# A fused attention, FFN and linear-attention kernel: a new step order in its linear phase, a split output projection and roots by Newton steps

## The chip, the cores and the metric

The kernel runs on one core of one Trainium2 chip. The metric is the device time of one execution in microseconds; lower is better. TensorE (PE) multiplies matrices and writes PSUM, VectorE (DVE), ScalarE (ACT) and GpSimd (POOL) do the elementwise work, SyncE (SP) issues DMAs. All engines run their own instruction queue in order and meet only at semaphores.

## The reference

A layer of four residual blocks on x of shape (2, 2048, 128): softmax attention, an FFN, a gated linear attention with 16 heads of width 64, and the FFN again. The change touches the third block:

```python
q = silu(x @ Wq); k = silu(x @ Wk); v = silu(x @ Wv)      # 16 heads of 64
q, k = l2norm(q), l2norm(k)
g = sigmoid(x @ Wf - dt_bias); beta = sigmoid(x @ Wb)
A = exp(-exp(A_log))
for t:                                                     # per batch and head
    o_t = (q_t @ state) * g_t
    state = A * state + beta_t * outer(k_t, v_t)
o = o * rsqrt(mean(o * o) + 1e-5) * norm_w
o = o * sigmoid(x @ Wg + bg)
x = x + o @ Wo
```

Here x is first normalized over its 128 channels.

## The kernel before

The linear phase (linear_phase, L1316 on) walks over NT = 16 tiles of 128 tokens, both batches at once, in steps m = -2 to 16. A step works on three tiles: it finishes tile m-1 (norm, output projection, residual), computes the recurrence of tile m, and prepares keys, values and queries of tile m+1. Within a tile a batch b has two chunks of 64 tokens; the recurrence inside a chunk is done by scores and attend, across chunks by recall (reading the 64x64 states) and update (products for the next state). Times in this text are in microseconds.

TensorE's jobs: by_feature makes q, f, g (f0 to f3 and so on, two 128x256 pieces each), by_token makes k, v (128x512). Both split their operands in a high and a low part and take three passes (three, L1443 to L1448). scores, attend, recall and update use quarters of the array (64x64); turn_k transposes k (64x128); sum_squares (128x32) adds the squares of q ("sq") and of the output u ("su"); turn_totals and turn_scales transpose; spread_scales (b0 to b3) spreads a head's scale over its features; project_out multiplies u with w_out in plain fp32 (L1588); turn_y and turn_x transpose.

The results go through four PSUM banks, ps0 to ps3, dealt out round by round in the order of the list in Ring: a job gets the bank of the job four places ahead of it, and free() lets TensorE wait until that job's reader is done. written() is the reader's wait for TensorE, taken() a wait for the reader. attend and recall share o_ps, update writes s_ps.

VectorE: decayed (scores times the decay table, L1735), new_state (L1797), gate_o (u = (f+1)o, L1783), gate_u (u = (gate+1)u, L1789), square_q (L1741), guard_q, add_totals and gather_totals (the sums of squares on their way to the root), scale_u (L1763), sum_k and guard_k (L1770, L1774), the layer norm's moments and normalize (L94 to L112), residual. ScalarE: silu of k, v, q (L1897, L1904), the tanh of f and g (L1916), squares (L1953, L1959), copies out of PSUM. GpSimd: decay_keys (L2079), decay_queries (L2086), fade (L2095), weigh_v (L2071), coefficients with a root by power of -0.5 (L2061), invert_totals with another such root and the split of its result into two parts (L2101 to L2106), low_x (L2052).

The order of each engine's work in a step is written out by hand in step(m) of that engine. TensorE's before:

```text
f0 be s0 f1 su k0 f2 sT k1 f3 v0 turn_k0 sq g0 k2 g1 k3 g2 sB g3 v1 b0-b3 attend v2 attend
project_out recall s1 v3 turn_y turn_x recall update q0 q1 attend turn_k1 attend q2 recall q3 recall update
```

(s0 and s1 are scores of batch 0 and 1, sT turn_totals, sB turn_scales, be the betas.)

## Time and profile before

| | us |
|---|---|
| median of 3 runs (914.35 to 917.34) | 914.47 |
| the profiled execution, its own time | 915.93 |
| its span, first to last instruction | 913.8 |
| PE busy | 841.7 (92%) |
| POOL busy | 636.4 (70%) |
| DVE busy | 548.9 (60%) |
| ACT busy | 511.6 (56%) |
| mean granted TensorE clock | 0.976 |

The linear phase fills the span from about 290 to the end; its steady steps lie between 345 and 830, and the last FFN overlaps its end. Busy times are averages over stages; what a step is bound by is read from a stretch of steps. In rows of the trace, DVE, ACT and POOL instructions that follow one another overlap by about 0.1 us, since an instruction's row reaches to its last write.

### The profile page before, as it was taken

The page shows a single profiled execution, that of the slowest core. Times are in us where ns is not written, and L with a number is a line of the kernel's source. Part 1 is how long each engine was busy: PE and PEld are TensorE (multiplying, and loading weights), DVE is VectorE, ACT ScalarE, POOL GpSimd, SP SyncE. Part 2 cuts the span into 40 slices and gives each one's busy share as a digit, 9 for nine tenths or more (in the row PEclk, how much of TensorE's full clock was granted, in tenths as well). Part 3 has the DMA queues.
Part 4 walks back from the last instruction along what each step waited for, and adds up shares of the span by engine and source line. Part 5 has one row for each costly group of instructions (what it writes and reads, how often), then busy time and mean ns, then how long its engine had stood idle before and what let it go on. Part 6 is the DMA issues. An engine that isn't in the chain of part 4 may idle for free. (4 is left out here: it accounts for less than half of the span.)

```text
span 913.8 us, 31013 instructions
## 1 busy us (share of the span) xinstructions
PE 841.7 (92%) x13152; PEld 717.5 (79%) x13152; DVE 548.9 (60%) x1247; ACT 511.6 (56%) x1105; POOL 636.4 (70%) x530
## 2 busy tenths in 40 slices
PE   4858998999797789999999999999999999998897
PEld 3648998899695678887888888888888888877786
DVE  3986566566684455655655655656556556666563
ACT  4745553565566636645646556566466467364354
POOL 3973211321455988898898898898898898988352
PEclk9998999999997889999999999999999999999999
DMA  5001000100100000000000000000000000000011
GB/s 189 25 13 34 25 12 1 31 19 1 25 1 1 1 3 3 3 3 3 3 3 2 3 4 2 3 4 2 3 3 3 4 2 3 4 1 3 3 36 57
DMA packets 19415, 12.36 MB, mean 14 GB/s; under 512 B 7760, under 2 KB 18768, under 8 KB 19024
## 3 DMA queue, kind: packets, MB, share of 16 engines
q1 hardware_dynamic: 19280, 10.39, 3.9%
q8 instruction: 105, 1.72, 0.8%
q14 instruction: 30, 0.25, 0.1%
HBM read 8.29 MB, written 2.10 MB: 11 GB/s over the span
## 5 line engine op out<-in xcount | busy, mean ns | idle before, releaser
L2101 POOL TENSOR_TENSOR la_scale<-la_scale,lt_mhalf 128x32 f32<-128x32 f32 x16 | 100.6, 6285 | 43.4 <-DVE la_scale L1756 43.4
L1446 PE MATMUL la_ps<-la_x_hi,w_hi 128*128 128x256 f32 x384 | 120.2, 313 | 0.4 <-ACT la_v L1897 0.4
L1447 PE MATMUL la_ps<-la_x_lo,w_hi 128*128 128x256 f32 x384 | 108.2, 282 | 0.0
L1448 PE MATMUL la_ps<-la_x_hi,w_lo 128*128 128x256 f32 x384 | 108.1, 281 | 0.0
L2061 POOL TENSOR_TENSOR la_coef<-la_ssk,lt_mhalf 128x32 f32<-128x32 f32 x16 | 87.0, 5440 | 13.8 <-DVE la_ssk L1774 13.8
L1797 DVE TENSOR_TENSOR lt_state<-la_s_ps,la_faded 128x512 f32<-128x512 f32 x62 | 42.3, 682 | 71.9 <-PE la_o_ps L1525 48.6
L1446 PEld LDWEIGHTS la_ps<-la_x_hi,w_hi 128*128 128x128 f32 x384 | 72.9, 190 | 16.0 <-issue 7.4
L531 POOL CAST at_q_hi<-qk_hi 128x128 fp32r<-128x128 f32 x32 | 9.4, 294 | 106.1 <-PE at_s_ps L572 103.6
L598 PE MATMUL at_o_ps<-V,at_probsT 128*128 128x128 f32 x544 | 75.1, 278 | 3.2 <-DVE at_probsT L507 2.0
L2079 POOL TENSOR_TENSOR la_k<-la_k,lt_decay_k 128x1024 f32<-128x1024 f32 x32 | 75.6, 2364 | 2.1 <-ACT n_xn L1953 2.1
L2086 POOL TENSOR_TENSOR la_qdT<-la_qT,lt_decay_q 128x1024 f32<-128x1024 f32 x32 | 76.3, 2384 | 0.0
L1447 PEld LDWEIGHTS la_ps<-la_x_lo,w_hi 128*128 128x128 f32 x384 | 73.2, 191 | 2.6
L713 ACT ACTIVATE at_probs<-at_s_ps,at_ntop 128x512 f32<-128x512 f32 (+2 forms) x80 | 49.0, 623 | 46.4 <-DVE at_ntop L655 46.2
L598 PEld LDWEIGHTS at_o_ps<-V,at_probsT 128*128 128x128 f32 x544 | 69.7, 194 | 6.3 <-DVE at_probsT L507 2.2
L1448 PEld LDWEIGHTS la_ps<-la_x_hi,w_lo 128*128 128x128 f32 x384 | 73.1, 190 | 0.0
L1763 DVE TENSOR_TENSOR la_u<-la_ps,la_u 128x512 f32<-128x512 f32 x64 | 39.7, 683 | 53.5 <-PE la_ps L1579 53.5
L1897 ACT ACTIVATE la_v<-la_ps 128x512 f32<-128x512 f32 x64 | 38.2, 599 | 51.1 <-PE la_ps L1448 50.9
L1735 DVE TENSOR_TENSOR la_pT<-la_ps,lt_decay 128x512 f32<-128x512 f32 x64 | 41.3, 686 | 41.7 <-PE la_ps L1490 41.7
L1916 ACT ACTIVATE la_f<-la_ps,lt_bias_f 128x256 f32<-128x256 f32 x128 | 53.5, 470 | 22.3 <-PE la_ps L1448 20.7
L2095 POOL TENSOR_TENSOR la_faded<-lt_state,lt_decay_s 128x512 f32<-128x512 f32 x62 | 64.7, 1043 | 0.1
L1904 ACT ACTIVATE la_qT<-la_ps 128x512 f32<-128x512 f32 x64 | 38.2, 599 | 46.7 <-PE la_ps L1448 46.3
L2071 POOL TENSOR_TENSOR la_v<-la_v,la_coef 128x1024 f32<-128x1024 f32 x32 | 62.0, 1938 | 1.3
(207 smaller groups left out, 2382.6 us busy)
## 6 DMA issues: line engine op xcount, KB each, us to landing
at_w_raw<-in_w SPq DMA_DIRECT2D x20, 128.0 KB, 2.2
X<-in_x SPq DMA_DIRECT2D x8, 256.0 KB, 2.9
out<-X SPq DMA_DIRECT2D x8, 256.0 KB, 2.3
qkv_cos<-in_cos SPq DMA_DIRECT2D x1, 1024.0 KB, 4.8
qkv_sin<-in_sin SPq DMA_DIRECT2D x1, 1024.0 KB, 7.0
lt_w_out<-in_w_out SPq DMA_DIRECT2D x4, 128.0 KB, 2.7
const<-in_const SPq DMA_DIRECT2D x1, 320.5 KB, 3.2
qkv_w<-in_w_qkv SPq DMA_DIRECT2D x1, 320.0 KB, 3.9
```

The costliest lines, as they stand in the source:

```text
L598: mm = eng.matmul(o_ps[n % 2][:, 0:P], probsT[:, (BLK[n] + j) % 2, t * P:(t + 1) * P], V[:, bass.ds(b * NT + kt, 1), :], start=(kt == 0), ...
L713: eng.activation(probs[:, n % 2, j * G:j * G + width], s_ps[:, k * G:k * G + width], ACT.Exp, bias=ntop[:, n % 2, 1:2], scale=1.0 / C, acc ...
L1446: eng.matmul(out, l_hi, r_hi, start=True, stop=False)
L1447: eng.matmul(out, l_hi, r_lo, start=False, stop=False)
L1448: return eng.matmul(out, l_lo, r_hi, start=False, stop=True)
L1916: act = eng.activation(where[:, c, :], ps[bank][:, r * W:(r + 1) * W], ACT.Tanh, bias=bias[:, c:c + 1], scale=0.5)
L2061: eng.tensor_tensor(coef[:, :], ssk[:, :], mhalf[:, :], ALU.pow).then_inc(s["coef_step"], 1)
L2071: eng.tensor_tensor(own, own, over_d(coef[:, b * H:(b + 1) * H]), ALU.mult).then_inc(s["vb_ready"], 1)
L2079: eng.tensor_tensor(own, own, over_d(decay_k[:, :]), ALU.mult).then_inc(s["kd_ready"], 1)
L2086: eng.tensor_tensor(by_chunk(qdT[:, b, :, :]), by_chunk(qT[:, :, tile(b)]), decay_q[:, :, :].unsqueeze(2).broadcast_to([P, NP, 2, L]), ALU ...
L2095: eng.tensor_tensor(faded[:, b, :, :], state[:, b, :, :], over_e, ALU.mult).then_inc(s["faded_second" if c else "faded_first"], 1)
L2101: eng.tensor_tensor(scale[:, :, :], scale[:, :, :], powers, ALU.pow).then_inc(s["scale_step"], 1)
```

## The change

- TensorE's step is put in another order: attend, turn_k, recall, scores, the squares of q and update stand in two groups, su is the third place where a part of the array is used. scores(m+1, 0) is done at the end of step m (scored).
- The ring's list follows that order.
- project_out takes three passes of high and low parts. w_out is split once; u is split each step by four high_u on ScalarE and four low_u on VectorE. u_hi and u_lo lie where sq and gate lie, so the squares of q go to the buffers of k and v (squares), and square_u and the tanh of g wait for "y".
- invert_totals is removed from GpSimd; inverse_roots on VectorE computes the root from an integer guess and three Newton steps, then the two parts: twelve instructions of 128x32, each waiting for the one before it.
- gate_u(m-1, 0) moves from step m-1 to step m; the orders of VectorE, ScalarE and GpSimd follow.

```diff
+I32 = mybir.dt.int32
+ROOT_GUESS = float(0x5F3759DF)
+ROOT_STEPS = 12
...
+        with ExitStack() as whole:
+            self.w_out = whole.enter_context(nc.sbuf_tensor("lt_w_out", [P, NP, P], F32))
+        self.w_out_lo = sb("lt_w_out_lo", [P, NP, P], F32R)
+        self.w_out_hi = sb("lt_w_out_hi", [P, NP, P], F32R)
...
-        sq = sb("sq", [P, NP, W])
+        with ExitStack() as before_scaling:
+            sq = before_scaling.enter_context(nc.sbuf_tensor("la_sq", [P, NP, W], F32))
+            gate = before_scaling.enter_context(nc.sbuf_tensor("la_gate", [P, NP, W], F32))
+        u_hi = sb("u_hi", [P, NP, W], F32R)
+        u_lo = sb("u_lo", [P, NP, W], F32R)
...
-            if job == "be" or job[0] in "kqv":
-                return exists(m + 1) if job != "sq" else exists(m)
+            if job in ("be", "s00", "s01") or job[0] in "kqv":
-        ring = Ring(("f0 be s00 s01 f1 su k0 f2 sT k1 f3 v0 kT0 kT1 sq g0 k2 g1 k3 g2 sB g3 v1 b0 b1 b2 b3 v2 y s10 s11 "
-                     "v3 yt xt q0 q1 kT2 kT3 q2 q3").split(), has, STEPS, BANKS)
+        ring = Ring(("f0 f1 su f2 sT f3 be k0 k1 v0 v1 kT0 kT1 s10 s11 sq sB k2 b0 b1 k3 b2 b3 v2 v3 q0 q1 q2 q3 y g0 g1 yt g2 g3 xt "
+                     "kT2 kT3 s00 s01").split(), has, STEPS, BANKS)
+
+        def scored(m, b):
+
+            return m - 1 if b == 0 else m
+
+        def squares(m, c):
+
+            own = (k if c < NP // 2 else v)[(m + 1) % 2][:, 1, :].rearrange("p (c t) -> p c t", c=NP // 2)
+            return own[:, c % (NP // 2), :]
...
             def scores(m, b):
-                if b == 0:
-                    for job in ("kT2", "kT3", "q3"):
-                        taken(eng, m - 1, job)
-                banks = [free(eng, m, f"s{b}{odd}") for odd in range(2)]
+                for job in ("kT2", "kT3") if b else ("kT0", "kT1", "q3"):
+                    taken(eng, m - 1, job)
+                at = scored(m, b)
+                banks = [free(eng, at, f"s{b}{odd}") for odd in range(2)]
...
             def turn_scales(m):
-                eng.wait_ge(s["scale_step"], 3 * m)
+                eng.wait_ge(s["scale_step"], ROOT_STEPS * m)
...
             def project_out(m):
-                for j in range(4):
-                    taken(eng, m, f"b{j}")
+                if m == 1:
+                    eng.wait_ge(s["w_lo_ready"], 1)
+                eng.wait_ge(s["ulo_ready"], 4 * m)
                 bank = free(eng, m, "y")
+                out = ps[bank][:, 0:W]
                 for c in range(NP):
-                    mm = eng.matmul(ps[bank][:, 0:W], w_out[:, c, :], u[:, c, :], start=(c == 0), stop=(c == NP - 1))
+                    eng.matmul(out, tables.w_out_hi[:, c, :], u_hi[:, c, :], start=(c == 0), stop=False)
+                    eng.matmul(out, tables.w_out_hi[:, c, :], u_lo[:, c, :], start=False, stop=False)
+                    mm = eng.matmul(out, tables.w_out_lo[:, c, :], u_hi[:, c, :], start=False, stop=(c == NP - 1))
...
                 prv, now, nxt = exists(m - 1), exists(m), exists(m + 1)
                 if now:
                     by_feature(m, "f0")
...
                     by_feature(m, "f1")
                 if prv:
                     sum_squares(m, "su")
...
                 if now:
                     by_feature(m, "f2")
                 if prv:
                     turn_totals(m)
...
                 if now:
                     by_feature(m, "f3")
                 if nxt:
+                    betas(m + 1)
+                    by_token(m, "k0")
+                    by_token(m, "k1")
                     by_token(m, "v0")
...
                     by_token(m, "v1")
...
                 if now:
                     attend(m, 0, 0)
                 if nxt:
...
+                    turn_k(m, 0)
                 if now:
                     attend(m, 0, 1)
...
                     recall(m, 0, 0)
                     scores(m, 1)
...
+                    sum_squares(m, "sq")
                     recall(m, 0, 1)
                 if now and nxt:
                     update((m, 0, 1), (m, 1, 0))
                 elif now:
                     update((m, 1, 0))
+                if prv:
+                    turn_scales(m)
                 if nxt:
...
+                    by_token(m, "k2")
+                if prv:
+                    spread_scales(m, 0)
+                    spread_scales(m, 1)
+                if nxt:
+                    by_token(m, "k3")
+                if prv:
+                    spread_scales(m, 2)
+                    spread_scales(m, 3)
+                if m == LAST:
+                    eng.wait_ge(up_read[1], B * LAST)
+                    ffn.turn(eng, 0)
+                if nxt:
+                    by_token(m, "v2")
+                    by_token(m, "v3")
+                    for j in range(4):
+                        by_feature(m, f"q{j}")
+                if prv:
+                    project_out(m)
+                if now:
+                    by_feature(m, "g0")
+                    by_feature(m, "g1")
+                if prv:
+                    turn_y(m)
+                if now:
+                    by_feature(m, "g2")
+                    by_feature(m, "g3")
+                if exists(m + 2):
+                    turn_x(m + 2)
                 if now:
                     attend(m, 1, 0)
                 if nxt:
                     turn_k(m, 1)
                 if now:
                     attend(m, 1, 1)
+                    recall(m, 1, 0)
+                if nxt:
+                    scores(m + 1, 0)
                 if m == LAST:
                     ffn.turn(eng, 1)
...
                 if now:
                     recall(m, 1, 1)
                 if now and nxt:
                     update((m, 1, 1), (m + 1, 0, 0))
+                elif nxt:
+                    update((0, 0, 0))
...
             def square_q(m):
                 taken(eng, m - 1, "q3")
-                for part in (slice(0, 4), slice(4, 8)):
-                    eng.tensor_tensor(sq[:, part, :], qT[:, part, :], qT[:, part, :], ALU.mult).then_inc(s["qsq_ready"], 1)
+                if m > 0:
+                    eng.wait_ge(up_full[1], B * m)
+                for half, where in enumerate((k, v)):
+                    part = qT[:, half * NP // 2:(half + 1) * NP // 2, :]
+                    own = where[(m + 1) % 2][:, 1, :].rearrange("p (c t) -> p c t", c=NP // 2)
+                    eng.tensor_tensor(own, part, part, ALU.mult).then_inc(s["qsq_ready"], 1)
...
+            def inverse_roots(m):
+
+                count = ROOT_STEPS * (m - 1)
+                taken(eng, m, "sT")
+                eng.tensor_scalar(root[:, :, :].bitcast(I32), scale[:, :, :].bitcast(I32), -0.5, ROOT_GUESS, ALU.mult,
+                                  ALU.add).then_inc(s["scale_step"], 1)
+                for turn in range(3):
+                    eng.wait_ge(s["scale_step"], count + 3 * turn + 1)
+                    eng.scalar_tensor_tensor(rest[:, :, :], root[:, :, :], -0.5, root[:, :, :], ALU.mult, ALU.mult).then_inc(s["scale_step"], 1)
+                    eng.wait_ge(s["scale_step"], count + 3 * turn + 2)
+                    eng.tensor_tensor(rest[:, :, :], rest[:, :, :], scale[:, :, :], ALU.mult).then_inc(s["scale_step"], 1)
+                    eng.wait_ge(s["scale_step"], count + 3 * turn + 3)
+                    eng.scalar_tensor_tensor(root[:, :, :], rest[:, :, :], 1.5, root[:, :, :], ALU.add, ALU.mult).then_inc(s["scale_step"], 1)
+                eng.wait_ge(s["scale_step"], count + 10)
+                high = parts[:, :, 0:H]
+                eng.tensor_copy(high, root[:, :, :]).then_inc(s["scale_step"], 1)
+                eng.wait_ge(s["scale_step"], count + 11)
+                eng.tensor_tensor(parts[:, :, H:2 * H], root[:, :, :], high.bitcast(F32), ALU.subtract).then_inc(s["scale_step"], 1)
...
+            def low_u(m, j):
+
+                eng.wait_ge(s["uhi_ready"], 4 * (m - 1) + j + 1)
+                part = slice(2 * j, 2 * j + 2)
+                eng.tensor_tensor(u_lo[:, part, :], u[:, part, :], u_hi[:, part, :].bitcast(F32), ALU.subtract).then_inc(s["ulo_ready"], 1)
...
                 prv, now, nxt = exists(m - 1), exists(m), exists(m + 1)
                 if now:
                     decayed(m, 0)
...
                 if prv:
+                    gate_u(m - 1, 0)
                     add_totals(m)
                     gate_u(m - 1, 1)
                     gather_totals(m)
+                    inverse_roots(m)
                 if now:
                     square_q(m)
                 if now and exists(m + 2):
                     normalize(m + 2)
...
                 if m == LAST:
                     ffn.moments(eng, 2)
                     ffn.moments(eng, 3)
+                if now:
+                    new_state(m, 0, 0)
+                    decayed(m, 1)
+                    guard_q(m)
                 if nxt:
                     sum_k(m + 1, 0)
+                if now and nxt:
+                    new_state(m, 0, 1)
                 if prv:
...
+                    scale_u(m, 0)
+                    scale_u(m, 1)
+                    low_u(m, 0)
+                    scale_u(m, 2)
+                    low_u(m, 1)
+                    scale_u(m, 3)
+                    low_u(m, 2)
+                    low_u(m, 3)
                 if nxt:
                     sum_k(m + 1, 1)
                     guard_k(m + 1)
...
                     ffn.normalize(eng, 0)
                     ffn.normalize(eng, 1)
                 if now:
...
                     gate_o(m, 0)
...
                 if m >= -1 and exists(m + 3):
                     norm.moments(eng, Tile(0, m + 3))
                 if m == LAST - 2:
                     ffn.moments(eng, 0)
+                    ffn.moments(eng, 1)
+                if prv:
+                    residual(m)
+                if m == LAST:
+                    ffn.normalize(eng, 2)
                 if now:
                     new_state(m, 1, 0)
                     gate_o(m, 1)
...
+                if now and nxt:
+                    new_state(m, 1, 1)
+                if m == -1:
+                    split_w_out()
...
+            def high_u(m, j):
+
+                taken(eng, m, f"b{j}")
+                part = slice(2 * j, 2 * j + 2)
+                eng.activation(u_hi[:, part, :], u[:, part, :], ACT.Copy).then_inc(s["uhi_ready"], 1)
...
                 prv, now, nxt = exists(m - 1), exists(m), exists(m + 1)
+                if prv:
+                    square_u(m - 1, 1)
                 if now:
...
+                    for j in range(4):
+                        gates(m, "f", j)
                 if nxt:
                     beta_tanh(m + 1)
...
                     silu_token(m, "k0")
...
                     silu_token(m, "k1")
...
                     silu_token(m, "v0")
+                    silu_token(m, "v1")
+                    square_k(m + 1, 0)
                     copy_kT(m, 0)
                     copy_kT(m, 1)
...
+                if prv:
+                    copy_scales(m)
                 if nxt:
                     silu_token(m, "k2")
...
+                    silu_token(m, "k3")
+                if prv:
+                    high_u(m, 0)
+                    high_u(m, 1)
                 if nxt:
...
                     silu_token(m, "v2")
                 if prv:
...
+                    high_u(m, 2)
+                    high_u(m, 3)
                 if nxt:
                     silu_token(m, "v3")
+                    square_k(m + 1, 1)
+                    for j in range(4):
+                        silu_q(m, j)
+                if m == -1:
+                    high_w_out()
+                if m == LAST:
+                    written(eng, m, "sq")
+                    ffn.copy_x(eng, 0)
+                if prv:
+                    copy_y(m)
+                if now:
+                    square_u(m, 0)
+                    for j in range(4):
+                        gates(m, "g", j)
...
                 prv, now, nxt = exists(m - 1), exists(m), exists(m + 1)
                 if now:
                     decay_queries(m, 0)
+                    decay_keys(m, 1)
+                if now and exists(m + 2):
+                    norm.inverse_roots(eng, Tile(0, m + 2))
                 if now:
...
+                    fade(m, 1, 0)
                     decay_queries(m, 1)
...
+                if m == LAST:
+                    ffn.roots(eng, 2)
+                    ffn.roots(eng, 3)
                 if nxt:
                     decay_keys(m + 1, 0)
+                if now and nxt:
+                    fade(m, 0, 1)
+                if nxt:
+                    fade(m + 1, 0, 0)
                     coefficients(m + 1)
                     weigh_v(m + 1, 0)
+                    weigh_v(m + 1, 1)
                 if now and nxt:
...
+                    fade(m, 1, 1)
                 if exists(m + 2):
                     low_x(m + 2)
```

## Rows read from the trace of the kernel before

**Rows 1.** Busy time of each engine in one stretch: busy us (xcount), granted clock

```profile
586.00:621.00 35.00, 34.52 (x712) 29.06 (x710) 20.51 (x34) 20.79 (x42) 31.57 (x20) 1.00 0.01 3
```

**Rows 2.** The list of waits, 430 to 830: us in total, times, longest

```profile
PE la_o_ps L1525 <- DVE lt_state L1797: 5.2, 11, 1.0
```

**Rows 3.** TensorE's timeline, 568 to 583: start, us, operation, operands, xcount

```profile
568.85 3.72 PE L1588 MATMUL la_ps<-la_u,lt_w_out 128*128 128x256 f32 x16
572.50 0.69 PE L1525 MATMUL la_o_ps<-la_qdT,lt_state 64*64 64x64 f32 x32
573.01 1.11 PE L1490 MATMUL la_ps<-la_qT,la_kT 64*64 64x64 f32 x64
...
581.06 0.28 PE L1447 MATMUL la_ps<-la_x_lo,w_hi 128*128 128x256 f32 x1
581.18 0.28 PE L1448 MATMUL la_ps<-la_x_hi,w_lo 128*128 128x256 f32 x1
581.38 0.69 PE L1525 MATMUL la_o_ps<-la_qdT,lt_state 64*64 64x64 f32 x32
582.01 0.38 PE L1446 MATMUL la_ps<-la_x_hi,w_hi 128*128 128x256 f32 x1
```

**Rows 4.** GpSimd's timeline, 569 to 605

```profile
569.77 5.44 POOL L2061 TENSOR_TENSOR la_coef<-la_ssk,lt_mhalf 128x32 f32<-128x32 f32 x1 [0.72 <-DVE la_ssk L1774]
...
577.48 1.05 POOL L2095 TENSOR_TENSOR la_faded<-lt_state,lt_decay_s 128x512 f32<-128x512 f32 x1
...
579.18 1.91 POOL L2071 TENSOR_TENSOR la_v<-la_v,la_coef 128x1024 f32<-128x1024 f32 x1
581.04 2.89 POOL L2079 TENSOR_TENSOR la_k<-la_k,lt_decay_k 128x1024 f32<-128x1024 f32 x1
...
585.83 2.38 POOL L2086 TENSOR_TENSOR la_qdT<-la_qT,lt_decay_q 128x1024 f32<-128x1024 f32 x1
...
604.68 5.44 POOL L2061 TENSOR_TENSOR la_coef<-la_ssk,lt_mhalf 128x32 f32<-128x32 f32 x1 [0.73 <-DVE la_ssk L1774]
```

**Rows 5.** ScalarE's timeline: two silus, and the copy of 128x513

```profile
578.08 1.21 ACT L1904 ACTIVATE la_qT<-la_ps 128x512 f32<-128x512 f32 x2 [1.81 <-PE la_ps L1448]
...
855.34 0.64 ACT L1283 ACTIVATE f_x_hi<-f_xT 128x513 fp32r<-128x513 f32 x1
```

**Rows 6.** VectorE's timeline, 580 to 605, and GpSimd's root at 591.52

```profile
580.34 1.83 DVE L1789 SCALAR_TENSOR_TENSOR la_u<-la_gate,la_u 128x1024 f32<-128x1024 f32 x1 [1.02 <-ACT la_sq L1959]
...
589.87 1.22 DVE L1789 SCALAR_TENSOR_TENSOR la_u<-la_gate,la_u 128x1024 f32<-128x1024 f32 x1
...
591.36 2.41 DVE L1741 TENSOR_TENSOR la_sq<-la_qT 128x1024 f32<-128x1024 f32 x2
...
603.18 1.21 DVE L1770 TENSOR_REDUCE la_ssk<-n_xn 128x16 f32<-128x1024 f32 x1
604.42 0.18 DVE L1774 TENSOR_SCALAR la_ssk<-la_ssk 128x32 f32<-128x32 f32 x1
...
591.52 6.34 POOL L2101 TENSOR_TENSOR la_scale<-la_scale,lt_mhalf 128x32 f32<-128x32 f32 x1 [2.31 <-DVE la_scale L1756]
```

**Rows 7.** GpSimd and VectorE in the start-up, 330 to 336

```profile
330.97 1.90 POOL L2071 TENSOR_TENSOR la_v<-la_v,la_coef 128x1024 f32<-128x1024 f32 x1
332.83 2.88 POOL L2079 TENSOR_TENSOR la_k<-la_k,lt_decay_k 128x1024 f32<-128x1024 f32 x1
...
331.02 2.92 DVE L1789 SCALAR_TENSOR_TENSOR la_u<-la_gate,la_u 128x1024 f32<-128x1024 f32 x1
```

**Rows 8.** The line of qkv_shift: duration ns min/median/max

```profile
L271 DVE SCALAR_TENSOR_TENSOR qkv_shift<-qkv_mv,qkv_rstd x8: 162/1239/1276, 6.4 to 46.9; 128x4 f32<-128x4 f32 x8
```

**Rows 9.** TensorE behind two waits, and its granted clock (last but two)

```profile
839.12 1.93 PE L1556 MATMUL la_ps<-la_sq,lt_pick 128*32 128x256 f32 x16 [2.44 <-DVE la_sq L1741]
...
335.58 1.14 PE L1525 MATMUL la_o_ps<-la_qdT,lt_state 64*64 64x64 f32 x32 [3.68 <-DVE lt_state L1797]
...
839.00:843.00 4.00, 3.88 (x28) 2.70 (x29) 1.85 (x12) 0.37 (x1) 4.00 (x1) 0.59 0.02 4
```

198 lines of the change are left out of this document (44 added, 154 removed).

## Prediction

> **What bounds the kernel now.** I read the table of stretches first. In the steady part of the linear phase, one 35.00 us stretch has TensorE busy 34.52, GpSimd 31.57, VectorE 20.51 and ScalarE 20.79 at full granted clock [rows 1]. One token tile takes 34.91 us, from one root of the coefficients to the next [rows 4]; I use 35.0. The list of waits comes next: TensorE's only real wait is the recall that needs a new state, 5.2 us over eleven steps [rows 2]. So the step is TensorE's issue time plus about 0.5 us, and GpSimd is the next bound. Then the timelines of each engine, to price every kind of job and to see what happens when two engines meet.
>
> **TensorE's own time, before any new wait.** A three-pass job of 128x256 pieces issues one matmul each 0.117 us, so a by_feature or by_token job costs 0.70; the gap from 581.18 to the recall at 581.38 (0.09 over the pitch), the recall's 0.63 instead of the 0.51 between 572.50 and 573.01, and the first matmul behind it, 0.38 long instead of 0.28, show what entering and leaving quarter-array work costs: 0.09 + 0.12 + 0.10 = 0.3 us a group [rows 3]. Before there are ten such groups a step (both scores, the two sums of squares, the turns of k, attends, recalls, updates, as the hand-written order has them). After there are three: 7 x 0.3 = 2.1 us less. project_out takes 3.65 (568.85 to 572.50); 24 passes of 0.117 are 2.8: 0.85 less. The wait of 0.5 is covered by scores and sum of squares (2.0 us against a new state of 0.7): 0.5 less. Added: a recall right behind an attend waits for its last matmul, twice about 0.2. Sum: 35.0 - 2.1 - 0.85 - 0.5 + 0.4 = 32.0; adding each job up by its pitch gives 32.3. I take 32.3. If the order had no other wait, 14 full steps (m = 1 to 14) would gain 38 us. It has others.
>
> **GpSimd and ScalarE totals.** The root of the totals leaves GpSimd, 6.34 us a step [rows 6]: 25 us of work remain. ScalarE gains four high_u. A 128x513 copy of SBUF to SBUF takes 0.64 and two silus of 128x512 1.21 [rows 5]: 0.6 each, 2.4 in all, 23 of the step. VectorE gains four low_u (half of a 1.2 us square each, 2.4) and twelve small root steps. The nearest row is the 128x32 guard of 0.18 us, started 0.03 behind the reduction [rows 6]: 0.21 each, 2.5 in all; bounds 0.1 and 0.3 (1.2 and 3.6). Totals: none above TensorE. What decides is who stands behind whom.
>
> **The collision.** VectorE's gate_u (two SBUF inputs, 128x1024) takes 1.22 alone and 1.83 at 580.34, where GpSimd's weigh_v of 579.18 still runs to 581.1 [rows 4, 6]. The start-up rows make the mechanism plain: weigh_v 330.97 to 332.87, gate_u 331.02 for 2.92 = 1.7 of waiting + 1.22, and GpSimd's next decay_keys, started 332.83, takes 2.88 = 1.0 of waiting + 1.9. All three are in [rows 7]. So these instructions exclude each other for their whole length, in turns: whoever comes second waits to the end. Small ones too: the 128x4 shift takes 0.162 at best and 1.24 in the median, in a stage where GpSimd adds 128x512 tiles all the time [rows 8]. A reduction, a PSUM-sourced addition and the root itself (a square runs its usual 1.2 within 591.52 plus 6.34, [rows 6]) do not show it.
>
> The Trainium skill, SBUF — State Buffer, section Who interferes with whom, says the same of the pair of ports that VectorE and GpSimd share: held for the whole instruction, by a VectorE instruction with two SBUF inputs or in a two-port mode. The other reading of the rows would be a shared bandwidth, by which gate_u loses half a microsecond and a 32-element step nothing; the sum by it is rival 3, 927 us, against 1021. I go by the rows, and the page lowers the chance of that rival.
>
> Before, the order on VectorE puts one gate_u and the squares of q into GpSimd's idle time or beside its root. After, gate_u(m-1,0), gate_u(m-1,1), twelve root steps, two squares of q and two normalizations follow one another at the start of the step, just where GpSimd has decay_queries 2.35, decay_keys 1.87, fade 1.0, decay_queries 2.35, decay_keys 1.87 back to back [rows 4].
>
> **The new step, placed by hand** (0 = TensorE starts f0; 0.27 from a matmul's issue end to its reader, 0.05 from a reader's end to TensorE, as in the rows).
> A 128x512 instruction is half a square, 0.6. The last recall is issued at -1.1; gate_o(m-1,1), new_state and decayed(m,0) then keep VectorE to 2.2. GpSimd holds with decay_queries(m,0) from 0.7 to 3.05, so gate_u runs 3.05 to 4.3 and add_totals ends at 4.7. turn_totals sits behind f2 (3.4) and waits to 4.75: 1.35 lost, f3 and all of k and v queued behind it. Now decay_keys to 6.15, second gate_u to 7.35, gather_totals 7.55: k1, whose bank that frees, waits 0.8. Roots: four until 8.4, then one each behind fade (9.4), decay_queries (11.75) and decay_keys (13.7), then GpSimd runs out, since its next fade waits for new_state(m,0,0); the last root step ends at 14.95. Squares of q to 17.4, normalize to 18.0, new_state(m,0,0) to 18.7.
> TensorE, with the 2.15 already lost, has done scores(m,1) at 13.5 and waits for the squares to 17.5: 4.0 lost. Queued behind it: the sum of squares, recall, update, sB and everything of the second half. Group one ends at 20.4 instead of 14.3 without the collision.
> Second half: b0 is written at 21.95; scale_u 0, 1; k3's silu ends 23.5; high 0, 1; low 0; scale 2 at 25.4; low 1; scale 3 at 26.6; high 3 at 27.2; v3, square_k, silu of q0 at 29.3. q0 waits for scale 2 (0.7), q1 for scale 3 (0.5), project_out for q0's bank (0.6), v2 0.15. From project_out on 11.5 us follow: the step ends at 40.9. GpSimd's own chain (guard_k at 30.2, root 5.44, product, two weigh_v 1.9, fade 1.04) ends there too and decides nothing more.
> **Clock.** After an idle 2.44 us on TensorE, from 839.12, the granted clock was 0.59 in the mean of 4 us, so 3.3 us of them at the lower level, 1.2 GHz; after an idle 3.68 a recall took 1.14 instead of 0.69 [rows 3, 9]. By that ratio 3.3 us of slow work lose 1.3. Both rows behind such a wait are slow; I take 1.4, bounds 0 and 2.2 (a slow stretch of 5.5 us). The 4.0 us hole should bring this in every step, and nothing hides it: b0 follows directly. Step: 42.3.
>
> **Ends.** m = 0 has no totals and already now waits 3.7 for a state [rows 9]: taken as equal, bounds -3 and +3. The last step has no k, v, q to lay over the chain scale, high, low; I place it 3 longer, and the tail 2 longer (the root of 5.44 becomes 2.5, the high and low parts add 2 to 3 before project_out, and the final FFN keeps its length). The split of w_out (one 128x1024 instruction of VectorE, 1.2, and one of ScalarE) lies in the start-up: 0, at most 2.
>
> **Sum.** 14 x (42.3 - 35.0) = 102; ends +5; 107. The profiled execution: span 913.8, own time 915.93; that is 1023 for its like. The median of the runs shown, 914.47, is 1.5 less. To it: 914.5 + 107 = 1021.
>
> **Rivals.**
> 1. Collision, but no fall of the clock: step 40.9, 14 x 5.9 + 5: 1002. For: the hole stands in a dense step. Against: both rows.
> 2. The small root steps don't wait (only the long ones do). Roots end at 10.1; squares behind decay_queries (11.65) and decay_keys (14.75): 16.0; the hole is 2.1 and the step 39.3 (with some clock 40): 979. Against: the 128x4 rows.
> 3. Sharing instead of exclusion: 0.5 on each of four long instructions; turn_totals waits 1.0, squares 0 to 1, state 0.4: step 35.9, 927.
> 4. Faster: GpSimd's batch is past before VectorE arrives, and the chain high, low, scale fits below k3 to q3. Place: the wait of q0, q1 and project_out for banks (1.8 us), turn_totals (0.45) and squares (0). It decides if GpSimd is idle by 2.2 of the step and each high_u and low_u takes at most 0.4: step 32.9, 14 x -2.1: 885. If only the collision is gone, the bank waits stay and the step is 34.7: 911, no change. For: TensorE's own 32.3, and its order has fewer switches. Against: GpSimd can't start weigh_v before guard_k, behind the last square of k, so its batch must spill over the step's start.
> 5. The change doesn't do what it says: if the three passes of project_out cost no less than 3.6, 14 x 0.85 = 12 more, 1033, inside the range.
>
> **Chances.** Forecast 0.60 (1005 to 1040); rival 1: 0.10; rival 2: 0.11; rival 3: 0.07; no collision, no change: 0.03; faster: 0.06; above 1045: 0.03. My placement errs by about 1 us a step, 14 us. The range 965 to 1045 holds the forecast with both clock bounds, rivals 1, 2 and 5. A measurement of this kernel tells about 0.5% (4.6 us) from no change. Faster by more: 0.07; within: 0.03; slower: 0.90.
>
> **What would show it.** Right: steps of 41 to 43 us; TensorE waiting about 4 us for la_sq (or its successor, the squares of q) in each step and 1 us for la_total; root steps on VectorE of 0.2 and of 1 to 2.3 us in turns; GpSimd's decay_queries and decay_keys lengthened; granted clock near 0.9 over the phase. Wrong: root steps all near 0.2 beside a busy GpSimd (rival 2), gate_u near 1.3 (rival 3), TensorE without idle time and steps near 33 (rival 4).

## The result: 1015 us against 915, and the profile after

| | before | after |
|---|---|---|
| median | 914.64 us (914.35 to 917.34) | 1015.04 us (1010.31 to 1016.14) |
| ratio | | 1.108, 95% interval 1.104 to 1.112 |
| profiled execution: own time, span | 915.93, 913.8 | 1014.22, 1012.2 |
| mean granted clock | 0.976 | 0.956 |
| one step of the linear phase, mean of twelve | 35.06 | 41.11 |

The forecast was 1021 (965 to 1045), slower. A step is read from one root of the coefficients to the next, on GpSimd. Each mean is taken over the same twelve steps, from the third such root to the fifteenth: from 369.55 to 862.86 after the change, from 358.94 to 779.71 before, where most steps take 34.9 and three take 35.4 to 35.7.

Two lines of the page first: the busy time of each engine, and the group of gate_u (columns: busy us and mean ns, then idle time before it).

```profile
PE 850.4 (84%) x13280; PEld 723.8 (72%) x13280; DVE 696.6 (69%) x1504; ACT 538.9 (53%) x1170; POOL 539.4 (53%) x481
...
L1829 DVE SCALAR_TENSOR_TENSOR la_u<-la_gate,la_u 128x1024 f32<-128x1024 f32 x32 | 60.9, 1902 | 0.0
```

TensorE is busy 84% of a span in which almost nothing but its own work used to end a step [rows 1], and gate_u has a mean of 1.90 us, where 1.22 is its time alone [rows 6].

The list of waits on TensorE over 450 to 900 us comes next (columns: engine, waiting instruction, what released it, total us, times, longest). Before, the longest line of this list was the recall that waits for a state, [rows 2].

```profile
PE la_ps L1575 <- DVE la_v L1756: 34.4, 11, 5.1
PE la_ps L1583 <- DVE la_total L1766: 7.3, 8, 1.3
...
PE la_s_ps L1558 <- issue: 6.0, 5, 1.5
...
PE la_ps L1509 <- issue: 2.4, 4, 0.9
PE la_ps L1465 <- DVE la_scale L1771: 1.5, 4, 0.6
```

The largest wait is that of the sum of squares (L1575) for the squares of q, which the change writes into the spare half of k and v (so it reads `la_v`): 34.4 us in eleven steps. The two lines with "issue" are idle time for which the profile shows no releaser, that is, no semaphore on which TensorE waited. They come back in the experiments.

VectorE's timeline over one step shows why the squares are late (columns: start us, us, engine, line, operation, out<-in, in brackets the idle time before it and its releaser). TensorE starts f0 at 627.12.

```profile
629.24 1.65 DVE L1829 SCALAR_TENSOR_TENSOR la_u<-la_gate,la_u 128x1024 f32<-128x1024 f32 x1
...
631.14 2.59 DVE L1829 SCALAR_TENSOR_TENSOR la_u<-la_gate,la_u 128x1024 f32<-128x1024 f32 x1
...
633.65 0.18 DVE L1771 COPY la_scale<-la_ps 128x32 f32<-128x32 f32 x1
...
634.76 0.92 DVE L1781 SCALAR_TENSOR_TENSOR la_rest<-la_root 128x32 f32<-128x32 f32 x1
...
635.71 2.30 DVE L1783 TENSOR_TENSOR la_rest<-la_rest,la_scale 128x32 f32<-128x32 f32 x1
...
638.05 1.87 DVE L1785 SCALAR_TENSOR_TENSOR la_root<-la_rest,la_root 128x32 f32<-128x32 f32 x1
640.95 1.22 DVE L1756 TENSOR_TENSOR la_k<-la_qT 128x1024 f32<-128x1024 f32 x1
```

And GpSimd in the same stretch:

```profile
627.40 2.41 POOL L2154 TENSOR_TENSOR la_qdT<-la_qT,lt_decay_q 128x1024 f32<-128x1024 f32 x1
...
629.77 2.88 POOL L2147 TENSOR_TENSOR la_k<-la_k,lt_decay_k 128x1024 f32<-128x1024 f32 x1
...
633.86 0.74 POOL L107 TENSOR_TENSOR n_rstd<-n_rstd,n_mhalf 128x2 f32<-128x2 f32 x1
634.57 1.06 POOL L2163 TENSOR_TENSOR la_faded<-lt_state,lt_decay_s 128x512 f32<-128x512 f32 x1
635.59 2.38 POOL L2154 TENSOR_TENSOR la_qdT<-la_qT,lt_decay_q 128x1024 f32<-128x1024 f32 x1
...
637.97 1.90 POOL L2147 TENSOR_TENSOR la_k<-la_k,lt_decay_k 128x1024 f32<-128x1024 f32 x1
```

The three long root steps are the three that meet fade, decay_queries and decay_keys: 634.76 + 0.92 ends at 635.68, where fade ends (635.63); 635.71 + 2.30 ends at 638.01, where decay_queries ends (637.97); 638.05 + 1.87 ends at 639.92, just past the end of decay_keys (639.87). The other nine take 0.18 to 0.19 each, one every 0.225. All have 128x32 operands. Four of the nine run beside an instruction of GpSimd too, but that one is a power (L107, 633.86 to 634.60), and it doesn't hold them. The other steps say the same: of the 156 root steps between 370 and 900 us forty are longer than 0.25 us, each of the forty ends 0.04 or 0.05 us behind a fade, decay_queries or decay_keys that was running when it began, and no short one has such a neighbour. The two gate_u, 1.65 and 2.59, meet decay_queries and decay_keys as the gate_u of [rows 7] met weigh_v.

TensorE at the end of that chain, and the granted clock of two such stretches (4 us from 601, where the wait was 2.69, and from 642.4, where it was 3.60; columns: stretch, length, busy us and instructions of each engine, clock, DMA share, GB/s):

```profile
643.45 0.64 PE L1575 MATMUL la_ps<-la_k,lt_pick 128*32 128x256 f32 x2 [3.60 <-DVE la_v L1756]
...
645.32 1.13 PE L1544 MATMUL la_o_ps<-la_qdT,lt_state 64*64 64x64 f32 x32
646.23 1.42 PE L1558 MATMUL la_s_ps<-la_v,la_k 64*64 64x64 f32 x64
```

```profile
601.00:605.00 4.00, 1.31 (x36) 0.70 (x32) 3.97 (x8) 0.00 (x0) 0.27 (x2) 1.00 0.00 0
642.40:646.40 4.00, 2.95 (x56) 1.81 (x60) 4.00 (x8) 0.00 (x0) 1.04 (x1) 0.64 0.00 0
```

An undisturbed recall reads 0.69 [rows 3]; here it is 1.13, and a matmul of the sum of squares is 0.64 where the step before has 0.41. The clock fell in the second stretch and not in the first.

### The profile page after: what moved, and what is told of

Its sections match the earlier page's. It is cut to its first block, busy times and chain, and to the rows that moved or that the text cites. A ratio compares the mean times of both kernels' runs of the same rounds, so it can differ in the third digit from the quotient of the medians.

```text
span 1012.2 us, 31561 instructions
## 1 busy us (share of the span) xinstructions
PE 850.4 (84%) x13280; PEld 723.8 (72%) x13280; DVE 696.6 (69%) x1504; ACT 538.9 (53%) x1170; POOL 539.4 (53%) x481
## 4 chain that ended last, share of the span: by engine, by line
PE 33%; DVE 23%; issue 9%; ACT 6%; POOL 1%; DVEq 0%; ACTq 0%; POOLq 0%
PE la_o_ps L1544 4%; DVE la_u L1829 4%; PE la_ps L1465 3%; PE la_s_ps L1558 3%; PE la_ps L1467 3%; PE la_ps L1466 3%; PE la_ps L1575 3%; DVE la_rest L1781 3%; PE la_o_ps L1528 2%; DVE la_rest L1783 2%; DVE la_u L1797 2%; PE la_ps L1509 2%; DVE la_root L1785 2%; PE la_ps L1609 2%; DVE la_v L1756 2%
## 5 line engine op out<-in xcount | busy, mean ns | idle before, releaser
L1465 PE MATMUL la_ps<-la_x_hi,w_hi 128*128 128x256 f32 x384 | 118.1, 308 | 9.3 <-DVE la_u L1797 8.7
L2163 POOL TENSOR_TENSOR la_faded<-lt_state,lt_decay_s 128x512 f32<-128x512 f32 x62 | 69.9, 1128 | 101.2 <-DVE lt_state L1837 101.2
L2000 ACT ACTIVATE la_scT<-la_ps 128x256 fp32r<-128x256 f32 x16 | 6.2, 384 | 133.3 <-PE la_ps L1590 133.2
L2147 POOL TENSOR_TENSOR la_k<-la_k,lt_decay_k 128x1024 f32<-128x1024 f32 x32 | 66.8, 2088 | 16.7 <-ACT n_xn L2027 16.7
L1575 PE MATMUL la_ps<-la_k,lt_pick 128*32 128x256 f32 x128 | 26.0, 544 | 47.9 <-DVE la_v L1756 47.9
L2033 ACT ACTIVATE la_sq<-la_u 128x1024 f32<-128x1024 f32 x32 | 33.8, 1056 | 55.3 <-DVE la_u L1823 55.3
L1829 DVE SCALAR_TENSOR_TENSOR la_u<-la_gate,la_u 128x1024 f32<-128x1024 f32 x32 | 60.9, 1902 | 0.0
L1465 PE MATMUL la_ps<-w_hi,la_x_hi 128*128 128x512 f32 x128 | 56.8, 443 | 2.7 <-DVE la_scale L1771 1.8
```

The costliest lines, as they stand in the source:

```text
L1465: eng.matmul(out, l_hi, r_hi, start=True, stop=False)
L1575: mm = eng.matmul(ps[bank][32 * quad:32 * (quad + 1), 0:W], pick[:, r if job == "sq" else 2 + r, :], squares(m, chunk) if job == "sq" else ...
L1829: eng.scalar_tensor_tensor(u[:, :, tile(b)], gate[:, :, tile(b)], 1.0, u[:, :, tile(b)], ALU.add, ALU.mult).then_inc(s["ug_ready"], 1)
L2147: eng.tensor_tensor(own, own, over_d(decay_k[:, :]), ALU.mult).then_inc(s["kd_ready"], 1)
L2163: eng.tensor_tensor(faded[:, b, :, :], state[:, b, :, :], over_e, ALU.mult).then_inc(s["faded_second" if c else "faded_first"], 1)
```

## The experiments

Twelve kernels were run beside the kernel before, whose times were 912.5 to 918.2 us. Three questions: what holds the root steps; what each of the three parts costs by itself; and what is left of the change when the lock is out of its way.

### roots_out: nine of the twelve root steps away

```diff
-                for turn in range(3):
-                    eng.wait_ge(s["scale_step"], count + 3 * turn + 1)
-                    eng.scalar_tensor_tensor(rest[:, :, :], root[:, :, :], -0.5, root[:, :, :], ALU.mult, ALU.mult).then_inc(s["scale_step"], 1)
...
```

> The changed kernel without the nine Newton instructions of the inverse roots on VectorE: the guess and the split into high and low part remain, so the scale that it writes is the raw guess and its output is not the reference's. Theory (VectorE and GpSimd exclude each other for a whole instruction, small ones too): the three roots that are left are done near 8.2 us of the step instead of 15, the squares of q and the normalization meet decay_queries and decay_keys instead and are ready near 12.5 to 13, before TensorE asks for them at 13.5. The 4 us hole goes, the step falls from 41.1 to about 37 us, the run to 955 to 965. Rival (a small instruction costs its 0.22 us and waits for nobody): nine times 0.22 = 2.0 us per step, 28 in all, 985 to 990, and the wait for the squares stays near 1 to 2 us. Rival (the hole has another cause, the squares' own length): no change, 1010 to 1015.

Measured: 970.93 us, ratio 1.062 (1.060 to 1.064), step 38.07 us. That is 44 us less, where nine steps of 0.225 come to 28 over the 14 steps, but 6 above the theory's 955 to 965. TensorE no longer waits for the squares in the steady steps; two waits are left, 3.2 us at 849 and 1.75 at 886. VectorE's and GpSimd's rows show where the rest stayed:

```profile
613.25 2.06 DVE L1756 TENSOR_TENSOR la_v<-la_qT 128x1024 f32<-128x1024 f32 x1
...
614.20 3.35 POOL L2147 TENSOR_TENSOR la_qdT<-la_qT,lt_decay_q 128x1024 f32<-128x1024 f32 x1
...
615.24 4.26 DVE L112 TENSOR_SCALAR n_xn<-X,n_mv,n_rstd 128x128 f32<-128x128 f32 x2
...
617.50 1.91 POOL L2140 TENSOR_TENSOR la_k<-la_k,lt_decay_k 128x1024 f32<-128x1024 f32 x1
...
619.42 0.68 DVE L1830 TENSOR_TENSOR lt_state<-la_s_ps,la_faded 128x512 f32<-128x512 f32 x1
```

With the roots gone the lock takes the next in the queue: a square of 1.22 becomes 2.06, and the two normalizations, 0.60 in a free stretch, become 4.26, so that new_state starts at 619.42, 14.3 us into the step.

### pool_late: one line of GpSimd's order moved

```diff
+                if now and nxt:
+                    fade(m, 0, 1)
                 if now:
                     fade(m, 1, 0)
                     decay_queries(m, 1)
...
                 if nxt:
                     decay_keys(m + 1, 0)
-                if now and nxt:
-                    fade(m, 0, 1)
```

> The changed kernel with one edit of order, on GpSimd alone: fade of tile 0's second chunk, which waits for VectorE's new_state(m, 0, 0), stands ahead of fade(m, 1, 0), decay_queries(m, 1) and decay_keys(m + 1, 0) instead of behind them. Same instructions on every engine. Theory (the two engines exclude each other): with GpSimd held back the twelve root instructions run at 0.22 us each, 2.6 in all, and the squares are ready near 12.6 us of the step instead of 17.4; TensorE's wait for them goes from 4 us to none, and so does the clock's fall behind it. Step 36.6 to 37, run 950 to 960. Rival (the roots are slow by VectorE's own load, or by each one's round trip through its semaphore): the wait stays, 1010 to 1016. Rival (GpSimd's later work turns into the new bound, decay_queries(m, 1) for q0's SiLU or guard_k for the coefficients): part comes back as waits of ScalarE or TensorE in the second half, 970 to 995.

Measured: 971.25 us, ratio 1.063 (1.060 to 1.066), step 38.15 us. Every instruction of the changed kernel is there, and 44 us are gone.

```profile
611.65 0.18 DVE L1777 TENSOR_SCALAR la_root<-la_scale 128x32 int32<-128x32 int32 x1
...
614.12 0.19 DVE L1790 TENSOR_TENSOR lt_parts<-la_root,lt_parts 128x32 fp32r<-128x32 f32 x1
...
615.36 1.22 DVE L1756 TENSOR_TENSOR la_v<-la_qT 128x1024 f32<-128x1024 f32 x1
...
617.77 2.05 POOL L2163 TENSOR_TENSOR la_faded<-lt_state,lt_decay_s 128x512 f32<-128x512 f32 x2 [5.39 <-DVE lt_state L1837]
```

The wait for the squares over 450 to 900 us:

```profile
PE la_ps L1575 <- DVE la_v L1756: 4.6, 2, 4.1
```

GpSimd is held from 612.4 to 617.77 (5.39 us) by the state, and twelve root steps take 2.66 us from 611.65 to 614.31 instead of about 7. The squares are done at 616.6, before TensorE asks at 617.57; its wait for them, 34.4 us in eleven steps after the change, is 0.6 in the same steps. The other 4.1 lie in the last step (m = 15), where the moved line doesn't run (a gate_u of 2.23 us and a root step of 2.13 show the lock again) and TensorE has no keys and values of a next tile to do first. The granted clock is 1.00 in the mean of 450 to 870 us, with one fall of 3.4 us at 495.7. The roots' own load or their semaphores, the first rival, would have left the time where it was. The step didn't reach the 36.6 to 37 I expected. By its time, 971, the run lies in the second rival's 970 to 995; what was left over is the subject of the later runs.

### plain_out: the projection undone

The four high_u and four low_u are left out, and the loop of project_out is that of before:

```diff
-                    eng.matmul(out, tables.w_out_hi[:, c, :], u_hi[:, c, :], start=(c == 0), stop=False)
-                    eng.matmul(out, tables.w_out_hi[:, c, :], u_lo[:, c, :], start=False, stop=False)
-                    mm = eng.matmul(out, tables.w_out_lo[:, c, :], u_hi[:, c, :], start=False, stop=(c == NP - 1))
+                    mm = eng.matmul(out, tables.w_out[:, c, :], u[:, c, :], start=(c == 0), stop=(c == NP - 1))
```

> The changed kernel with its output projection undone: 16 passes of w_out by u in plain float32 as before, without the four copies of the high part on ScalarE and the four subtractions of the low part on VectorE. The roots and the step order stay as changed. Theory: TensorE's projection goes from 2.9 back to 3.7 us (+0.8 a step), but 2.6 us of VectorE and 2 us of ScalarE leave the stretch in which q0, q1 and the projection wait, which is worth 1.5 us or a little more; the hole ahead of the squares stays. Step 0.7 us shorter, run 1002 to 1008. Rival (the split is hidden): only the 0.8 is seen, 1022 to 1028. Rival (VectorE is the bound of the whole step): all 2.6 us come back, less 0.8: 985 to 992.

Measured: 1007.9 us, ratio 1.102 (1.099 to 1.105), step 40.82 us. As expected: in this order the three passes cost about 7 us more than they give, 0.3 to 0.5 a step. The intervals of the two ratios just touch (1.105 and 1.104), so the size is uncertain.

### before_newton, before_split, order_only, order_pow: each part by itself

before_newton puts `inverse_roots(m)` behind `gather_totals(m)` on VectorE in the kernel before, and takes `invert_totals(m)` off GpSimd:

```diff
                     gather_totals(m)
+                    inverse_roots(m)
...
-                if prv:
-                    invert_totals(m)
```

> The kernel before with one part of the change alone: the inverse roots as twelve VectorE instructions right behind gather_totals, and none on GpSimd. Step order and output projection as before. Theory: in the kernel before the squares of q end at 593.8 us and TensorE asks for them at 593.92, so they have next to no slack; twelve instructions of 0.22 us push them by 2.6, and decay_queries and fade, which GpSimd can now start earlier, collide with the roots for up to 2.4 more. Step 2.4 to 4.8 us longer, run 948 to 980. Rival (GpSimd's 6.3 us root was what held its queue, so taking it off pays back at least as much): 905 to 918. Rival (small instructions behind a slack that other waits make up): within 5 us of 915.

Measured: 1031.03 us, ratio 1.128 (1.126 to 1.129), step 43.27 us. The direction and the mechanism held, and the size was far off: this small part alone costs more than the whole change. The waits on TensorE over 450 to 900 us, and VectorE and GpSimd:

```profile
PE la_ps L1561 <- DVE la_sq L1746: 60.8, 10, 6.2
```

```profile
598.62 2.40 POOL L2112 TENSOR_TENSOR la_qdT<-la_qT,lt_decay_q 128x1024 f32<-128x1024 f32 x1
...
599.34 2.76 DVE L1813 SCALAR_TENSOR_TENSOR la_u<-la_gate,la_u 128x1024 f32<-128x1024 f32 x1
...
600.98 2.02 POOL L2121 TENSOR_TENSOR la_faded<-lt_state,lt_decay_s 128x512 f32<-128x512 f32 x1
...
602.23 0.80 DVE L1767 TENSOR_SCALAR la_root<-la_scale 128x32 int32<-128x32 int32 x1
...
605.43 4.06 DVE L1746 TENSOR_TENSOR la_sq<-la_qT 128x1024 f32<-128x1024 f32 x2
605.57 2.84 POOL L2105 TENSOR_TENSOR la_k<-la_k,lt_decay_k 128x1024 f32<-128x1024 f32 x1 [2.57 <-ACT n_xn L1979]
```

I had priced the roots at 2.6 us and their own collisions at up to 2.4. What I left out is that the root on GpSimd, 6.34 us [rows 6], had been a shelter. While GpSimd waited for the totals gate_u ran alone in 1.22, and beside the power the two squares took 1.2 each [rows 6]: a power doesn't exclude VectorE. The other way round it does wait: the root of 6.34 us started 0.16 behind the first square and is 0.90 longer than the 5.44 of a power that starts with VectorE's instruction out of the way [rows 4, 6], and in best3, below, the same root takes 5.42 in the steps where it starts clear of the squares. With the root gone GpSimd's next three instructions move up: gate_u takes 2.76 (1.54 more), the squares 4.06 for two (1.65 more, where I had put nothing), the first root step 0.80, and the eleven others 2.5. Between the end of gate_u and the end of the squares lie 7.4 us (602.1 to 609.49) instead of 2.7 (591.09 to 593.77, [rows 6]). TensorE waits 6.1 us in each step, and the clock falls behind it: 0.927 over the run.

before_split puts the three-pass projection alone into the kernel before:

```diff
                     for j in range(4):
                         scale_u(m, j)
+                    for j in range(4):
+                        low_u(m, j)
...
+                if prv:
+                    high_u(m, 0)
...
```

> The kernel before with one part of the change alone: the output projection in three passes of high and low parts (the low part takes u's own place in memory, since there is no room for both; four copies on ScalarE and four subtractions on VectorE stand behind the four scale_u). Order and roots as before. Theory: the pass count gives TensorE 0.8 us back, but scale_u and low_u are 5 us of VectorE from 565.9 on, and decay_keys excludes them for up to 0.5: the projection starts near 571.2 instead of 568.85, a wait of 2.0 to 2.4 us. Step 1.2 to 1.9 us longer with the clock's part, run 931 to 945. Rival (the split is hidden behind attend and v2): 0.8 a step less, 902 to 906. Rival (sizes cancel): 912 to 918.

Measured: 965.55 us, ratio 1.053 (1.050 to 1.056), step 38.56 us, where I had 36.1 to 36.8.

```profile
PE la_ps L1597 <- DVE la_u_lo L1780: 26.3, 11, 2.4
...
PE la_o_ps L1532 <- DVE lt_state L1814: 8.2, 8, 1.5
```

The wait for the low parts is 2.4 us a step, as placed. Not placed: the wait for the state, 8.2 against 5.8 us before, and the clock, which falls at this wait in nine of the twelve steps (0.958 over the run against 0.976). The three steps that begin under a fall of 6.8 us took 40.4 to 40.8 us; the nine others, behind a fall of 3.4 us or none, took 37.8 to 38.1. So a short fall costs nothing that shows here (the three steps without one wait 1.3 to 1.5 us for the state instead) and a long one 2.6 to 3. Of the 3.5 us a step 1.65 are the wait less the passes saved, 0.2 the state, about 0.7 the long falls; 1.0 is left that I can't divide.

order_pow is the changed kernel with the roots back on GpSimd, order_only has the plain projection as well, so the step order alone. In both `invert_totals(m)` stands behind the normalization's roots:

```diff
                 if now and exists(m + 2):
                     norm.inverse_roots(eng, Tile(0, m + 2))
+                if prv:
+                    invert_totals(m)
```

> The changed kernel with its roots undone alone: the totals are inverted by one power instruction and two small ones on GpSimd, right behind the roots of the normalization there, and VectorE has no root step. Step order and three-pass projection as changed. Theory (the lock, and a power on GpSimd does not hold it): squares of q are done by 10.5 us of the step, the hole of 4 us is gone; what is left is la_total 1.35, the bank of k1 0.8 and about 2 in the second half. Step 36 to 37, run 930 to 950. Rival (the step order itself is what costs, the roots don't matter): 1000 to 1015. Rival (GpSimd's 6.3 us more make its queue the bound, with decay_queries(m, 1) and decay_keys(m + 1, 0) late by as much): 960 to 985.

> The changed kernel with both other parts undone: roots by one power instruction on GpSimd, projection in 16 plain passes, so the new step order alone. Theory: against order_pow (998, step 39.9) the low_u that stood between scale_u 1 and 2 and beside decay_queries and decay_keys are gone, which held TensorE's scale passes 1.9 us a step and the banks of q0 and q1 about 1; the plain projection costs 0.7 more. Step 37.3 to 38, run 955 to 970: the order alone is still 4 to 6% slower than the kernel before, by GpSimd's batch at the start of the step and by the waits without a shown cause inside the quarter-array work (0.1 us a step before, 1.2 to 1.5 after). Rival (the order by itself is neutral or better, the two other parts carry the whole loss): 900 to 925. Rival (the split was hidden in order_pow): 1000 to 1010.

Measured: order_pow 998.2 us, ratio 1.089 (1.087 to 1.092), step 39.87; order_only 1008.15 us, ratio 1.103 (1.100 to 1.105), step 40.85. Both are misses: I had 950 and 970 at most. The squares are in time in both, and another chain takes their place. From order_only:

```profile
559.41 2.37 POOL L2111 TENSOR_TENSOR la_qdT<-la_qT,lt_decay_q 128x1024 f32<-128x1024 f32 x1
...
561.74 1.89 POOL L2104 TENSOR_TENSOR la_k<-la_k,lt_decay_k 128x1024 f32<-128x1024 f32 x1
...
563.60 1.03 POOL L2120 TENSOR_TENSOR la_faded<-lt_state,lt_decay_s 128x512 f32<-128x512 f32 x1
...
564.74 0.69 DVE L1817 TENSOR_TENSOR lt_state<-la_s_ps,la_faded 128x512 f32<-128x512 f32 x1 [3.68 <-POOL la_faded L2120]
565.35 2.47 DVE L1777 TENSOR_TENSOR la_u<-la_ps,la_u 128x512 f32<-128x512 f32 x4
```

The root (6.34 us, started at 551.45 beside a square) pushes decay_queries, decay_keys and fade back; fade ends at 564.6, new_state(m, 0, 1) waits 3.68 us for it, and queued behind new_state on VectorE are the four scale_u, for which TensorE's third spread then waits 2.31 us. Of the waits over 450 to 870 us the two largest are:

```profile
PE la_ps L1600 <- DVE la_u L1777: 19.4, 10, 2.7
PE la_ps L1467 <- ACT la_gate L1948: 10.6, 11, 1.0
```

This is the rival I had put at 960 to 985 in order_pow's expectation, and it cost 13 more than that; the time is nearer to the other rival there, that the order itself is what costs (1000 to 1015). The rows show both at once: the time is lost in GpSimd's queue, and it is the new order that gives this queue no room. That order_only is 10 us slower still (in its rival's 1000 to 1010), and not faster, is read from the second line: with the plain projection gate_o waits for the projection's end instead of for low_u, the squares of u and the gates of ScalarE come behind it, and TensorE waits for a gate's bank, 10.6 us in eleven steps, where order_pow's list has 0.5, once. GpSimd's order was written for a queue without the root: fade(m, 0, 1) stands last in its batch, and the step has nothing to spare there.

So the three parts don't add: the order alone costs 93 us, the roots alone 116, the split alone 50, and all three together 100. The order with the root on GpSimd loses by GpSimd's queue; with the roots on VectorE that chain is short again, and the lock takes its place.

### best, best_pow: the lock out of the way, and VectorE's order mended

```diff
                 if prv:
-                    gate_u(m - 1, 0)
                     add_totals(m)
-                    gate_u(m - 1, 1)
                     gather_totals(m)
                     inverse_roots(m)
+                    gate_u(m - 1, 0)
+                    gate_u(m - 1, 1)
...
                     scale_u(m, 1)
-                    low_u(m, 0)
                     scale_u(m, 2)
-                    low_u(m, 1)
                     scale_u(m, 3)
+                    low_u(m, 0)
+                    low_u(m, 1)
```

> The kernel of pool_late with three more edits of order and nothing else. VectorE: add_totals, gather_totals and the roots stand ahead of the two gate_u, and the four scale_u ahead of the four low_u. ScalarE: v2 and v3 ahead of the second pair of high_u, square_k(m + 1, 1) behind the first SiLU of q. TensorE: turn_k(m, 1) behind the recall, so that new_state(m, 1, 0) has 0.6 us more. Theory (what was left over TensorE's own 32.3 us in pool_late's step of 38.1 are waits behind VectorE's order: la_total 0.8, la_scale 0.4, banks held by scale_u 0.9 to 1.8, the state 0.4, and about 0.8 inside the update): most of them go, the step is 33.5 to 34.5, the run 893 to 908, under the kernel before. Rival (TensorE's own time in the new order is nearer 34.5 than 32.3): 35 to 36 us, 915 to 930, no gain on before. Rival (another lock takes the place of the old: the four low_u beside decay_queries and decay_keys): 36 to 37, 930 to 945.

> The kernel of best, but with the roots as one power instruction on GpSimd behind the normalization's roots, as in the kernel before, instead of twelve instructions on VectorE. Theory: the root on GpSimd ends near 11 us of the step and is asked for near 15, and VectorE has 2.6 us less in the first half, so TensorE sees neither: within 6 us of best, 890 to 910. That would say that moving the roots to VectorE gains nothing where GpSimd's queue has room. Rival (GpSimd, at 31 to 32 us of work in a step of 34, becomes the bound): 4 to 20 us slower than best. Rival (root steps on VectorE were still in the way in best): 5 to 15 us faster than best.

Measured: best 940.16 us, ratio 1.026 (1.022 to 1.030), step 35.44; best_pow 940.63 us, ratio 1.027 (1.024 to 1.030). Another 31 us against pool_late by order alone, and nothing between roots on VectorE and roots on GpSimd, once neither is in the other's way: best_pow came out as expected against best, both 30 to 50 us above what I had for them. Neither rival fits alone. The step is the first one's (35 to 36; TensorE's own time in the new order is above 32.3 us), and the run is above that rival's 930 and within the second's 930 to 945. The shortest of best's steps is 34.72. The squares still wait at times (10.1 us in seven places of 450 to 870 us, one of 4.9 in the last step), and there is the idle time without a shown cause, taken up next; with them the mean is 35.44.

### best2, best3n, best3: is the rest to be had?

best2 breaks the long stretches of 64x64 work (v1 ahead of the sum of squares, g3 and the turn of x ahead of the scores), puts the squares ahead of both gate_u, and mends the last step:

```diff
                     scores(m, 1)
+                if nxt:
+                    by_token(m, "v1")
+                if now:
                     sum_squares(m, "sq")
...
```

> The kernel of best with edits of order alone. TensorE: v1 stands between scores(m, 1) and the sum of squares, g3 and the turn of x between turn_k(m, 1) and scores(m + 1, 0), so that neither stretch of quarter-array work runs longer than about 200 matmuls; ScalarE and the banks follow. VectorE: the squares of q and the normalization directly behind the roots, the two gate_u behind them. Last step: GpSimd held back as in the others, the moments of the FFN behind new_state; values(1) of the FFN ahead of the last projection, where TensorE waited 2.9 us for low_u. Theory A (long runs of 64x64 matmuls outrun the supply of instructions, which is what the idle time without a shown cause is: 0.8 us a step in best, 1.5 in pool_late, 0.1 in the kernel before): that idle time falls under 0.3 a step. Theory B (it comes with the place in memory or in time, not with the length of the runs): it stays near 0.8. The wait for the squares (0.4 in most steps of best, 4.9 in the last) is gone in both. Step 34.3 to 34.9 by A, 34.9 to 35.4 by B; run 905 to 918 by A, 918 to 928 by B.

Measured: 928.03 us, ratio 1.013 (1.010 to 1.017), step 35.68; five of its twelve steps are 34.73 to 34.75, as between these two rows of GpSimd:

```profile
577.38 5.44 POOL L2135 TENSOR_TENSOR la_coef<-la_ssk,lt_mhalf 128x32 f32<-128x32 f32 x1 [2.58 <-DVE la_ssk L1816]
...
612.12 5.44 POOL L2135 TENSOR_TENSOR la_coef<-la_ssk,lt_mhalf 128x32 f32<-128x32 f32 x1 [2.58 <-DVE la_ssk L1816]
```

The steps are no shorter than best's. What best2 gained is at the end: the root that closes its twelve steps stands at 791.86 us, 2.05 later than in best, and its span ends 6.2 us earlier (926.8 against 933.0).

Idle time without a shown cause on TensorE, summed over 450 to 830 us: 0.9 us in two pieces before, 9.5 in ten after, 15.8 in 21 in pool_late, 10.0 in 16 in best, 8.7 in eight in best2, 4.7 in six in best3n, 7.1 in seven in best3. One such piece of best2, and one of after:

```profile
624.01 1.02 PE L1558 MATMUL la_s_ps<-la_v,la_k 64*64 64x64 f32 x50 [1.69 <-issue]
```

```profile
668.56 1.02 PE L1558 MATMUL la_s_ps<-la_v,la_k 64*64 64x64 f32 x50 [1.22 <-issue]
```

Shorter stretches halve the number of pieces, and those that are left are longer; the sum falls by an eighth in best2 and by up to a half in best3n, not to the 0.3 a step of theory A. The 0.8 us a step of best2 is theory B's, and its time is at the edge of B's range. best_pow, with TensorE's order just as in best, has 13.6 us in 21 pieces, so differences of a few us here say little.

The traces show one thing more. The pieces come at fixed places of TensorE's stream. Counted in matmuls from the program's first, one comes ahead of matmul 6010 in before (at 517.33 us), after (546.41) and all eight other kernels with the new order and the three passes. All 125 pieces of these kernels and before_newton between 450 and 830 us lie within two matmuls of a whole multiple of 125.35 matmuls from there, where chance would put one in 25. (plain_out and order_only, with other matmuls in the step, have 35, all within eight.) And 139 of the 160 stand inside a job of 64x64 matmuls. So theory B had the place right, and the length of a stretch is not the cause by itself. What costs the time at these places stays open: a supply of instructions in portions would fit, and so would the rarity of the pieces in the kernel before, where the same matmuls are strewn over ten places; no run varies it alone.

best3n moves fade(m + 1, 0, 0) behind both weigh_v; best3 has the roots on GpSimd besides:

```diff
                 if nxt:
-                    fade(m + 1, 0, 0)
                     coefficients(m + 1)
                     weigh_v(m + 1, 0)
                     weigh_v(m + 1, 1)
+                    fade(m + 1, 0, 0)
```

> The kernel of best2 with one edit of order on GpSimd: fade(m + 1, 0, 0) stands behind the coefficients and both weigh_v instead of ahead of them, so that it doesn't lie beside the low_u. Theory (the lock): the four low_u take 2.4 to 3.2 us instead of 4.0 and the projection no longer waits 0.6 to 0.8 us for them; a full step that has no idle time without a shown cause falls from 34.74 to 34.0 to 34.2, the run from 928 to 917 to 921. Rival (the low_u wait for the high_u of ScalarE, not for GpSimd): no change, 926 to 930.

> The kernel of best3n with the roots back on GpSimd (one power instruction and two small ones behind the normalization's roots, where its queue is idle for 7 us), none on VectorE. Theory: VectorE does the squares and both gate_u 2.7 us earlier, new_state(m, 0, 0) is there before the recall (0.45 us a step in best2), the root on GpSimd ends 2 us before it is needed. Step 33.6 to 33.9 where there is no idle time without a shown cause, run 907 to 915: level with the kernel before or just under it. Rival (GpSimd's queue, at 31 us of 34, now runs late into the fades): 918 to 935, slower than best3n.

Measured: best3n 932.82 us, ratio 1.019 (1.016 to 1.022); best3 932.1 us, ratio 1.017 (1.015 to 1.020). No gain on best2 in either. By their times both lie above the theories; best3n lies above its rival too, and best3 within its rival's 918 to 935, but no slower than best3n. The wait for low_u went, as expected (8.3 us in ten steps of best2, one last wait of 2.9 in best3n), and other waits took its place. best3n's rows, and a line of its waits:

```profile
622.60 2.05 POOL L2169 TENSOR_TENSOR la_faded<-lt_state,lt_decay_s 128x512 f32<-128x512 f32 x2
...
624.75 0.69 DVE L1839 TENSOR_TENSOR lt_state<-la_s_ps,la_faded 128x512 f32<-128x512 f32 x1 [1.26 <-POOL la_faded L2169]
...
625.36 1.28 DVE L1748 TENSOR_TENSOR la_pT<-la_ps,lt_decay 128x512 f32<-128x512 f32 x2
```

```profile
PE la_ps L1575 <- DVE la_pT L1748: 8.2, 8, 1.3
```

The moved fade now stands ahead of fade(m, 1, 1): new_state(m, 1, 1) waits 1.26 us for it, decayed comes behind, and the sum of squares of the next step waits for its bank, 8.2 us in eight steps; the recall's wait for a state grows too, from 4.6 to 8.3 us. No version beats the kernel before; the best of them is 1.3% above it.

## Why the prediction was right, step by step

**Direction and mechanism.** The collision was the likeliest case, and it is shown, not only argued: the same instructions in another order on GpSimd alone (pool_late) take 44 of the 100 us away and leave every root step at 0.18 to 0.20 us but for one in each of the last two steps. Rival 3 (sharing of bandwidth) and rival 2 (small steps don't wait) fall with the rows above, where a 128x32 step ends with the neighbour's instruction three times in a row. Rival 5 falls too: the three passes take about 2.7 us (2.8 forecast). The rule of the Trainium skill, SBUF — State Buffer, section Who interferes with whom, that the pair of ports is held for the whole instruction, agrees with the 0.92, 2.30 and 1.87 us here, and not with the power, which leaves VectorE free for its 5.44 us though the rule names no exception; there the measurement decides. The prediction read it as taking no part at all; it does wait for VectorE when it starts, so of the 6.34 us that were to leave GpSimd 0.90 were such a wait.

**The placement.** In the step from 627.12: the copy of the totals ends at 6.7 us (7.55 forecast), three root steps meet fade, decay_queries and decay_keys in that order as forecast, the last ends at 13.9 (14.95), the squares near 16.2 (17.4). The whole chain came one microsecond early; the order and the partners were right.

**The terms of the sum**, a step each:

| term | forecast | measured |
|---|---|---|
| TensorE's own time | 32.3 | about 33.6 |
| wait of turn_totals | 1.35 | 0.6 to 0.7 |
| bank of k1 | 0.8 | 0.3 where it shows |
| hole ahead of the squares | 4.0 | 3.0 (1.6 to 3.6 in ten steps) |
| second half | 1.95 | 1.3 to 1.5 |
| idle time without a shown cause | 0 | 1.0 |
| clock | 1.4 | 0.9 by the rows, 0.3 by the steps |
| step | 42.3 | 41.1 |

Own time: best2's undisturbed steps of 34.74 still hold 0.64 us of waiting for low_u and 0.37 for the state, which leaves 33.7; the medians of best's stretches from one matmul to the next, over eight steps, add up to 33.6. The term of the sum that was mis-sized is the price of the switches. The prediction's own sum without it is 35.0 - 0.85 - 0.5 + 0.4 = 34.05, so seven fewer switches gave 0.35 to 0.45 us and not 2.1. The second half is 8.83 us from the turn of the scales to project_out, against 7.2 to 8.0 in best (7.55 where it still waits 0.2 there).

**The clock** was taken too high as well. I took 1.4 for every step. The fall came in eight of the twelve, after waits of 2.69 to 3.60, and stayed out after waits of 1.61, 2.16, 2.69 and 3.04, so the length of the wait alone doesn't settle it. Where it came, the sum of squares took 1.87 us instead of 1.02, the recall 0.91 instead of 0.52, the update up to 1.35 instead of 1.08: 1.25 to 1.5 us, near the forecast, times 8/12 is 0.9. But the eight steps that hold a slow stretch average 41.26 us and the four without 40.82, only 0.44 apart, since the waits behind vary by as much. The place without the clock, 40.9, was met within 0.1 us, by errors that cancel: own time and unexplained idle time 2.3 too low, the four waits together 2.7 too high.

**The ends.** 14 steps of 6.05 us more are 85, against 102 forecast. The measured difference is 100.4, so the ends carry 16 and not 5 (14 by the profiled spans, which differ by 98.4). ScalarE's copies of y divide it: the first stands at 361.77 before and at 371.76 after, the last at 881.98 and 975.66, the spans end 31.8 and 36.5 us behind that. So 10.0 lie ahead of the first copy (most of one full step's 6 is in them, which leaves about 4 for the start, forecast 0 with 3 either way), and 4.7 behind the last; the last step, with 3.4 us of waiting for low_u, has the rest. In the tail the final FFN now waits 3.4 us in two places for its gated output, which it did not before: I had taken it as equal. The forecast was 6 too high, as the sum of 17 too much in the steps and 11 too little at the ends; that it came so near is in part luck. (A slip: the list of chances adds up to 0.91 slower and 0.06 faster, where the last line has 0.90 and 0.07.)

**What the prediction didn't see.** The parts don't add. The prediction spoke of the root that leaves GpSimd as 6.34 us of relief. before_newton shows the other side: that root, and GpSimd's wait ahead of it, were where VectorE could run freely. And the order itself, which the prediction took to be good for 38 us if nothing collided (885 to 911 in rival 4), is still 13 (best2) to 24 us (best) slower than the kernel before with most collisions moved away. Of the 43 us between best2 and the 885 about 31 are its own time, 1.4 us a step above the forecast, and the unexplained idle time of 0.8.

## What to carry to other kernels

In this kernel VectorE and GpSimd exclude each other on elementwise work from SBUF for whole instructions (a power on GpSimd excepted), so a chain of n tiny VectorE instructions is not n times its 0.2 us: it hands the lock over at each step, and costs the length of whatever GpSimd has queued. Before moving work between the two, list what GpSimd does in the same stretch, and count an instruction that leaves GpSimd as a loss of shelter as well as a gain, if it is one beside which VectorE runs free. Holding GpSimd's batch back behind one wait it needs anyway was worth 44 us here, with no instruction changed.

## What the runs showed of the hardware that was not expected

- A 128x32 step (0.19 us alone) waits out the neighbour's instruction as a 128x1024 one does: 0.92, 2.30 and 1.87 us. In roots_out two normalizations of 128x128 took 4.26 instead of 0.60.
- A power on GpSimd (5.44 us for 128x32) doesn't exclude VectorE: two squares ran in 2.4 beside it before [rows 6], and in 4.06 with it gone (before_newton). It does wait at its start for a VectorE instruction that is under way: 6.34 us beside a square, 5.42 to 5.44 alone.
- In the new order, with dense stretches of 64x64 matmuls, TensorE has idle time that no semaphore explains: 0.1 us a step before, 1.0 after, 0.4 to 0.8 in best2, best3n and best3, in pieces of up to 1.9 us. The pieces of all these kernels stand on one grid of places, 125.35 matmuls apart; the cause is open.
- After the change the granted clock fell to half, the lower level of 1.2 GHz, after an idle 2.69 us in three steps and stayed up after 2.69 and 3.04 in others. In before_newton, with 6.1 us of waiting in each step, it fell in every one.
